# Matmuls of a constant tile in front of TensorE's long waits, in a Mamba-style block with eight experts

## The reference

```
mod = (silu(c) @ wmod) -> sa, ca, ga, sb, cb, gb           # per sequence; |ga|, |gb| at least 0.25
h   = layernorm(x) * (1 + ca) + sa
zxbcdt = h @ in_proj.T                                     # 256 z, 384 xBC, 2 step sizes
for each direction (forward, backward):
    xBC = silu(causal_conv4(xBC)); dt = softplus(dt + bias)
    state = state * exp(dt * A) + dt * x B^T;  y = state C + D * x     # 2 heads of 128, 64 states
    y = rmsnorm(y * silu(z)) * norm_w
x = x + ga * ((y_forward + y_backward) @ out_proj.T)
h = layernorm(x) * (1 + cb) + sb
expert = argmax(h @ gate_w.T + gate_b + expert_bias)       # one of 8 for each token
x = x + gb * (relu(h @ w1[expert] + b1) @ w2[expert] + b2) # 128 -> 512 -> 128
```

## Time and profile before

| | |
|---|---|
| median of 3 runs | 460.34 us |
| lowest and highest | 454.33, 462.12 us |
| profiled execution | 461.37 us |
| its span | 459.4 us |
| mean granted TensorE clock | 0.948 |
| TensorE busy | 380.9 us, 2890 matmul instructions |
| VectorE, ScalarE, GpSimd busy | 360.5, 290.1, 306.0 us |

### The profile page before, as it was taken

How to read it: one execution, slowest core, us unless ns; L and a number is a source line. 1 busy time by engine, 2 the same in 40 slices (tenths; PEclk the granted TensorE clock), 3 DMA queues, 4 the chain that set the end, 5 groups by cost and what they waited for, 6 DMA issues and landing times.

```text
span 459.4 us, 10205 instructions
## 1 busy us (share of the span) xinstructions
PE 380.9 (83%) x2890; PEld 341.1 (74%) x2890; DVE 360.5 (78%) x1081; ACT 290.1 (63%) x823; POOL 306.0 (67%) x464
## 2 busy tenths in 40 slices
PE   1998799788999899798998898999841299999980
PEld 1756688678888687687898688889731299999980
DVE  5668679999979898979798887987885078777761
ACT  2767879586799887787777789896410134444330
POOL 4745875564975979589898888695656035656642
PEclk9999999898999999999999999999975589999996
DMA  8100000000000000010101100050114668887740
GB/s 233 62 12 3 0 1 3 0 1 0 3 1 1 3 1 0 1 49 0 48 3 46 49 1 1 1 184 1 49 47 155 171 175 231 233 222 222 204 121 1
DMA packets 21574, 29.18 MB, mean 64 GB/s; under 512 B 4092, under 2 KB 14588, under 8 KB 21392
## 3 DMA queue, kind: packets, MB, share of 16 engines
q1 hardware_dynamic: 16240, 20.75, 16.4%
q0 software_dynamic: 2832, 6.50, 3.9%
q10 hardware_dynamic: 2448, 1.29, 1.0%
HBM read 20.97 MB, written 8.01 MB: 63 GB/s over the span
## 4 chain that ended last, share of the span: by engine, by line
PE 25%; DVE 19%; issue 13%; ACT 8%; SPq 7%; DMA 4%; POOL 2%; ACTq 1%; another core or an unknown queue 0%; POOLq 0%; DVEq 0%
DVE bank L1684 4%; PE bank L1291 3%; SPq L530 3%; DMA zs<-routed_rows 3%; PE bank L1311 2%; PE bank L1307 2%; PE bank L1284 2%; SPq L539 2%; PE bank L1303 2%; PE bank L1492 2%; DVE st L1730 2%; SPq L523 2%; PE bank L1271 1%; DVE cx L1696 1%; DVE xn L1575 1%
## 5 line engine op out<-in xcount | busy, mean ns | idle before, releaser
L621 POOL TENSOR_TENSOR accb<-accb,prod 128x512 f32<-128x512 f32 x48 | 61.3, 1277 | 39.9 <-ACT accb L916 36.4
L1684 DVE SCALAR_TENSOR_TENSOR bank<-raw,cw,bank 128x512 f32<-128x512 f32 x96 | 72.1, 751 | 2.3 <-ACT bank L926 0.9
L823 POOL DMA_INDIRECT out_dram<-raw x39 | 38.1, 976 | 37.8 <-DVE raw L2094 14.3
L657 POOL TENSOR_SCALAR lseg<-strict,av 128x128 f32<-128x128 f32 x128 | 47.9, 387 | 7.9 <-DVE av L1643 4.5
L1291 PE MATMUL bank<-skip,cx 128*128 128x128 f32 x256 | 41.9, 287 | 10.4 <-DVE st L1730 9.9
L1165 ACT ACTIVATE raw<-bank 128x128 f32<-128x128 f32 x39 | 10.8, 277 | 58.5 <-PE bank L1481 37.1
L1291 PEld LDWEIGHTS bank<-skip,cx 128*128 128x128 f32 x256 | 34.5, 196 | 13.4 <-DVE st L1730 12.8
L2071 DVE TENSOR_SCALAR raw<-bank,zs 128x128 f32<-128x128 f32 x78 | 23.8, 346 | 25.5 <-PE bank L1492 25.4
L965 ACT ACTIVATE xt<-bank,dtv 128x128 f32<-128x128 f32 x128 | 39.3, 360 | 7.1 <-PE bank L1272 5.3
L1509 PE MATMUL bank<-raw 128*128 x312 | 43.6, 284 | 0.0
L1492 PE MATMUL bank<-raw,zs 128*128 128x128 f32 x312 | 43.0, 282 | 0.0
(11 more groups left out here) (233 smaller groups left out, 1089.3 us busy)
## 6 DMA issues: line engine op xcount, KB each, us to landing
zs<-in_w_dram SPq DMA_DIRECT2D x39, 258.0 KB
zs<-routed_rows SPq DMA_DIRECT2D x39, 130.0 KB
raw<-in_w_dram SPq DMA_DIRECT2D x1, 2048.0 KB, 8.3
xs<-in_u_dram SPq DMA_DIRECT2D x3, 512.0 KB, 8.7
routed_rows<-padrow ACTq DMA_DIRECT2D x6, 130.0 KB
out_dram<-raw POOLq DMA_INDIRECT x39
xs<-in_u_dram SPq DMA_DIRECT2D x2, 256.0 KB, 4.8
routed_rows<-rows,rowat POOLq DMA_INDIRECT x32
```

Source lines behind the costliest of these rows:

```text
L621: pool.tensor_tensor(accb[:, :], accb[:, :], prod[:, :], ALU.add).then_inc(s_tapb, 1)
L657: last = pool.tensor_scalar(lseg[:, Q % LA, h, :], strict[:, d, :], av[:, b, col(d, h, t)], 1.0, ALU.mult, ALU.mult)
L823: pool.indirect_dma_start(out_rows, bass.IndirectOffsetOnAxis(ap=tok[:, s % 4, :].bitcast(mybir.dt.uint32), axis=0), ob[:, s % 4, :], None ...
L1684: dve.scalar_tensor_tensor(out=acc(S, g)[:, :], in0=raw[:, g, c0:c0 + BLK], scalar=cw[:, d, g, k:k + 1], in1=acc(S, g)[:, :], op0=ALU.mult ...
```

## The change

A helper `keep_warm(area, count)` issues `count` matmuls of `ones` by `ones` into an area of PSUM that the next real matmul overwrites. It waits for nothing. 286 of them are added: 56 in the prologue, 56 at five kinds of place in the stream (chunks 4, 48, 10 and 14, the second batch's prefix sums, one pair of transposes), 67 between the steps of the tail and 107 in three lots behind the last ranks. Two waits on signals that come early are added (`s_modc`, `s_yz` at 63), since bank 0 and bank 4 are used as areas, and the wait for `s_tabv` moves ahead of the wait for the pads. No instruction is removed.

```diff
+WARM_TABLE, WARM_SCATTER, WARM_ROWS = 48, 45, 14
+WARM_ENTRY = {4: 12, 48: 8}
+WARM_DECAY = {10: 12, 14: 9}
+WARM_LOADS, WARM_MOD, WARM_TURN, WARM_BLOCK = 16, 8, 8, 4
...
+            def keep_warm(area, count):
+
+                for _ in range(count):
+                    pe.matmul(area[:, 0:P], ones[:, :], ones[:, :], start=True, stop=True, skip_group_check=True)
...
             def sums(b):
                 u = USE["pfx", b]
                 take(pe, u)
+                if b == 1:
+                    keep_warm(side(u), 9)
                 pe.wait_ge(s_a, b + 1)
...
             def prepare(Q):
...
                 tx, sg = bank[0], bank[2 + Q % 2]
+                if Q in WARM_ENTRY:
+                    keep_warm(sg, WARM_ENTRY[Q])
                 if j == 0:
                     pe.wait_ge(s_gx, NH * (S + 1))
                     pe.wait_ge(s_cc, S + 1)
...
                 if Q >= 2:
                     pe.wait_ge(s_m, Q - 1)
+                if Q in WARM_DECAY:
+                    keep_warm(sg, WARM_DECAY[Q])
                 pe.matmul(sg[:, DI:DI + P], bb[:, S % 2, c0:c0 + P], cc[:, S % 2, c0:c0 + P],
...
             def y_turn(g, m):
                 u = USE["yT", g, m]
                 take(pe, u)
+                if (g, m) == (2, 0):
+                    keep_warm(side(u), 6)
                 pe.wait_ge(s_ysum, 2 * g + m + 1)
...
+            pe.wait_ge(s_fill0, 1)
+            keep_warm(bank[7], WARM_LOADS)
             pe.wait_ge(s_csbc, 1)
+            keep_warm(bank[7], WARM_MOD)
             pe.wait_ge(s_mod, 16)
             for m in range(2):
                 last = pe.matmul(bank[0][:, m * B:(m + 1) * B], wm[:, m * DM:(m + 1) * DM], csil[:, :], start=True, stop=True)
             last.then_inc(s_pmod, 1)
+            keep_warm(bank[7], WARM_TURN)
             pe.wait_ge(s_const, 2)
             turn(0)
+            keep_warm(bank[7], WARM_BLOCK)
             pe.wait_ge(s_win, 32)
             project(0, 2)
             project(0, 0)
+            pe.wait_ge(s_modc, 1)
             turn(1)
             first_step_sizes(0)
+            keep_warm(bank[0], WARM_BLOCK)
             turn(2)
+            keep_warm(bank[0], WARM_BLOCK)
             first_step_sizes(1)
+            keep_warm(bank[0], WARM_BLOCK)
             turn(3)
+            keep_warm(bank[0], WARM_BLOCK)
             first_step_sizes(2)
+            keep_warm(bank[0], WARM_BLOCK)
             first_step_sizes(3)
             project(0, 1)
...
+            pe.wait_ge(s_yz, NCH - 1)
+            keep_warm(bank[4], 6)
             ranks(LASTG - 2)
+            keep_warm(bank[4], 4)
             out_proj(LASTG, 0)
+            keep_warm(bank[4], 6)
             y_turn(LASTG, 1)
+            keep_warm(bank[4], 4)
             out_proj(LASTG, 1)
+            keep_warm(bank[4], 4)
             h2_turn(LASTG - 1)
+            keep_warm(bank[4], 5)
             logits(LASTG - 1)
+            keep_warm(bank[4], 9)
             ranks(LASTG - 1)
+            keep_warm(bank[4], 16)
             h2_turn(LASTG)
+            keep_warm(bank[4], 4)
             logits(LASTG)
+            keep_warm(bank[4], 9)
             ranks(LASTG)
+            keep_warm(bank[4], WARM_TABLE)

             pe.wait_ge(s_yz, NCH)
             for key in (("o", LASTG, 0), ("o", LASTG, 1), ("h2", LASTG), ("lg", LASTG), ("rk", LASTG)):
                 wait_free(pe, USE[key])
+            pe.wait_ge(s_tabv, 1)
+            keep_warm(bank[4], WARM_SCATTER)
+            pe.wait_ge(s_pad_act, 16 * len(ACT_PADS))
+            keep_warm(bank[4], WARM_ROWS)
             pe.wait_ge(s_wf, 16)
             pe.wait_ge(s_b2, 10)
-            pe.wait_ge(s_tabv, 1)
```

## The result

The changed kernel takes 466.10 us (median of 4 runs, 464.04 to 466.40) against 459.43 (4 runs, 454.33 to 462.12): a ratio of 1.018, 95% interval 1.014 to 1.023. The result is inside the 2% that I called no difference, on the slower side, 0.5 us above the forecast of 465.6. The profiled execution took 466.26 us, span 464.5, mean granted clock 0.987 (0.948 before).

What follows compares the result with a forecast made beforehand. It took TensorE, busy 83% of the span, as the bound, with clock falls in a few stretches. Its terms summed to +5.3 us on the profiled 461.37, 466.7, hence 465.6 against the 460.34 median; range 453 to 475.

Steps and rivals of the forecast that it cites:

- Price of a fill: Each filling call is one f32 matmul of two instructions, 0.2225 us warm and 0.43 cold.
- Rival 1: A fill costs one instruction, so the tail's fills mostly hide: -6.9 us, 453.4 us; chance 0.14.
- rival 3: The fills don't raise the clock at all, and the time is about 510 us; chance 0.03.
- Tail, +9.9: Last output transposes to first slot: 174 fills add up in order on TensorE, moving the slot from 364.12 to 374.1.
- Slots, -2.7: First expert slots start warm with all rows landed: 3.7 us in place of 6.48; later slots stay TensorE-bound at 2.0 each.
- Prefix sums, +2.0: Second batch's prefix sums: nine fills behind the bank wait are covered by nothing, +2.0 us, bounds 0 to +2.0.
- Prologue, -1.9: Prologue, 56 fills: projections stay at 12.54 but run warm, last step sizes come 1.9 us earlier; bounds -3.3 to +0.5.
- rival 2: Prologue clock falls back at the first transposes, five blocks of fills cost 8.6 us: +10.5, 476.1 us; chance 0.11.
- Stream, -2.0: Stream fills: -0.5 at chunk 4, -0.3 at chunk 10, -1.2 at chunk 14; 0 at 185 us and chunk 48.
- Part 1's bound: Skill page's ramp penalty below 1% of span: at most 4.6 us to win, against 6.6 of clock gains carried.

Runs made afterwards that it cites:

- second profile of before: The kernel before, unchanged, profiled once more: span 451.0 us at mean clock 0.938, against 459.4 at 0.948 in its first profile.
- e8: The changed kernel with its 107 lot fills made of a bf16 tile of ones, same counts: 459.59 us, ratio 1.004 to the kernel before.
- e11: e9 plus nine fills before the first prefix sums and four before the first start rows: 457.48 us, ratio 1.001 to the kernel before.
- e3: The kernel before with only the 56 prologue fills, added waits kept: 459.40 us, ratio 1.000.
- e4: The kernel before with only the tail's 67 + 107 fills: 469.11 us, ratio 1.019.
- fitted versions: Changed kernels with the lots behind the last ranks cut from 48, 45, 14, first to 24, 34, 9 (e2): 459.66 us, ratio 1.002.
- e9: Changed kernel with lots of 24, 34, 9 and eight fills ahead of the second prefix sums' bank wait, not nine behind: 456.51 us, ratio 0.998.
- e7: e11 with 31 fills in place of 67 between the tail's steps and lots of 22, 30, 12: 456.79 us, ratio 1.002.
- e2: The changed kernel with lots of 24, 34, 9 in place of 48, 45, 14 behind the last ranks: 459.66 us, ratio 1.002.

## Why the prediction was right, point by point

The total was right (465.6 forecast, 466.10 measured), and so were the price of a fill and what it does in the tail and at the second prefix sums, which make most of it. That the sum agrees so closely is in part luck:

| us | forecast | first profile of before to after |
|---|---|---|
| up to chunk 0's output | -1.9 | -0.57 |
| stream up to chunk 24 | -2.0 | -1.75 |
| second prefix sums | +2.0 | +2.01 |
| rest of the stream | 0 | -1.47 |
| tail up to the first slot | +9.9 | +10.60 |
| slots | -2.7 | -3.72 |
| sum | +5.3 | +5.1 |

The -1.47 and some 0.9 of the slots belong to the first profile and not to the fills: the second profile of before has 167.57 us there, less than the changed kernel's 168.04, and waits for no rows from the fifth slot on. They covered what the prologue did not give. Against the second profile the change costs 13.5 us, and over all runs 1.8% where I had 1.1%.

- **Price of a fill.** 0.2225 assumed, 0.2247 measured (348.90 to 372.94 is 24.04 us for 107). By the Trainium skill's 81 ns in a stream ("TensorE: Matmul & The Clock Gate", "Back-to-back issue gap") a call would be an estimated 0.16 us; the trace does not agree: 0.112 us for each f32 instruction, and 0.059 for bf16 in e8, which is near the 56 ns that the page gives for the isolated case. Rival 1 (one instruction a fill) is ruled out by x572, rival 3 by the clock line.
- **Tail, +9.9.** Measured +10.6 from the last transposes to the first slot. The order was as told: no gap on TensorE, rows landed 8.4 us before it read them, the last ranks late by 2.3 (I said 2). The excess is 174 times 0.0022, 0.4, and small gaps.
- **Slots, -2.7.** Measured 6.48 to 3.64, -2.84 (the row at 370.60 belongs to the fourth slot, not to the third as I wrote). I added that nothing absorbs the rest; the later slots gave 0.9 more, since from the fifth on TensorE waited 1.91 us for rows in the first profile of before and 0.67 us in all after the change. The second profile of before has no such waits, so this is no gain of the fills.
- **Prefix sums, +2.0.** Measured 6.68 against 4.67. But in both profiles of before the clock did not fall there. In three others without those fills it did (7.74 to 7.76), and against these the nine gain 1.0.
- **Prologue, -1.9: the step that failed.** The step sizes did come 1.4 earlier, the projections took 1.8 in place of 3.55, rival 2 did not come. But chunk 0's output came only 0.57 earlier: TensorE waited 2.23 us at 29.63 and 0.88 at 33.18 for VectorE's tables, the clock fell, and from 33.6 to 39 us everything took twice as long. e11, which fills both waits, has no fall there and still needs 35.12 us to chunk 0 where the changed kernel needs 35.55, so the fall itself is worth 0.4. Worse, were one slow prologue: the second profile of before has its last step sizes at 22.67 without any fill. In three other executions without prologue fills chunk 0 comes at 41.98, 42.08 and 42.13; in the eight with the 56 alone at 42.67 to 45.03. Against these the prologue's fills are a loss of some 2 us in the profiles (e3's ratio of 1.000, 0.996 to 1.004, can't tell it), most of it the first 24, which I had put at nothing by leaving the projections at 12.54. Their end hangs on when the clock rises, and that varies: 48 instructions took 6.97 to 8.53 us. The same page of the Trainium skill says in its part 1, "What's actually happening", that the number of cold matmuls at a kernel's start changes from run to run; this agrees with the 48 instructions and with the two profiles of before, and I hadn't used it.
- **Stream, -2.0.** From chunk 0's output to chunk 3's -0.98 and to chunk 5's -1.24 (I had -0.5 at chunk 4), chunk 10 nothing (-0.3), chunks 13 to 16 -0.6 (-1.2), together -1.75 to chunk 24. VectorE is busy 9.9 of 10 us there and passes little of TensorE's gain on. Of the places at 185 us and chunk 48 I wrote that the clock never fell. In e3 and e4 chunks 30 to 31 take 7.3 us in place of 4.8, in no profile with the six fills at 185, so these are worth up to 2.5 us in some executions. The eight before chunk 48 cost 0.65: from chunk 45's output to chunk 48's it is 10.08 to 10.10 us in the second profile of before, e3 and e4, and 10.73 to 10.75 in the ten kernels that have them; I had 0, with a bound of 0.5.
- **Part 1's bound.** By the Trainium skill's "<1% of a typical kernel span" ("TensorE: Matmul & The Clock Gate", part 1) at most an estimated 4.6 us were to be won. Against the second profile of before the segments show 1.9 in the stream and 1.7 in the slots, 3.6 together: within its bound, and not the 6.6 that I carried.

My expectations of the fitted versions failed by the same step: they took the first profile as before, and its stream and prologue are late ones. What stays open: why the padding rows' last transfer takes 3.0 us in one execution and 5.5 in another, and why, of the 3 us by which the slots of the first profile of before are longer than those of the second, 1.0 remains beside the 1.9 that TensorE waits for rows. A version with only the chunks' fills, the moved sums' fills and a short lot, without the prologue's and the chain's, was not run; from the segments it would be the one to try. None of the versions run is measurably faster than the kernel before; the nearest is e9 at 0.998 (0.995 to 1.001).

## What to carry to other kernels

A filling matmul on an in-order engine is free only up to the end of the wait that it covers. Count it in instructions of its own type, put it ahead of the wait and not behind it, and make a lot shorter than the shortest wait seen: one that is too long is paid in full on the critical path (8.4 us here), one that is missing costs a slow start of 1.6 to 2.8 us. Before counting on the clock, profile the kernel more than once: where the clock falls, and so what a fill can win, changed here from one execution to the next by as much as the whole gain. And follow a hand-over to its end before counting on it: ranks that were 3.5 us earlier in e7 brought the rows 0.6 us.

## What the runs showed of the hardware that I had not expected

- Making TensorE faster made its clock fall elsewhere: with the prologue's fills the stretch from 33 to 39 us went from 1.00 to 0.50, and with fills in the two waits ahead of it (e11) it is back at the full level.
- Mean granted clock and time hardly go together in this kernel: 451.0 us at 0.938, 459.4 at 0.948, 455.1 at 0.992.
- A bf16 fill takes 0.059 us against 0.225 for an f32 one. In e8 107 of them in three bursts, 2.95 and 3.70 us apart, did not hold the clock that 67 f32 ones with one gap of 1.16 us held in e2; whether the type or the gaps made the difference was not separated.
- The clock's rise in the first 30 us differs between executions of one program: in the earlier trace rows it was slow past 21.85 us, in the second profile fast at 16.23 and slow again from 20 to 26 us.
